# Three halvings before the column sums, quarter loads of the first two tiles, and eleven context widenings on GpSimd

## What is computed

```python
def fake_quant(x, scale, zp):
    q = jnp.clip(jnp.round(x / s + z), 0.0, 255.0)
    return (q - z) * s

x = x + tanh(g_xattn[0]) * matmul(fake_quant(layernorm(x)), fake_quant(ctx))
x = x + tanh(g_ffn[0]) * ffn(layernorm(x))     # base product, plus LoRA weighted by a top-2 router
```

## Time and profile before

| | us |
|---|---|
| median of three executions | 1054.52 |
| lowest, highest | 1052.64, 1057.77 |
| the profiled execution | 1053.84 |
| span of the profiled execution, first to last instruction | 1052.1 |
| PE busy over the span | 1018.3 (97%) |
| DVE busy | 761.2 (72%) |
| ACT busy | 482.2 (46%) |
| POOL busy | 270.8 (26%) |

### The profile page before, as it was taken

One profiled execution on the slowest core, in us unless ns is written; L12 is line 12 of the kernel. 1 busy time (PEld: TensorE's weight loads), 2 busy tenths in 40 slices (PEclk: granted clock), 3 DMA queues, 4 the chain that ended last, 5 costly groups with the idle time before them and its releaser, 6 DMA issues.

```text
span 1052.1 us, 13343 instructions
## 1 busy us (share of the span) xinstructions
PE 1018.3 (97%) x5048; PEld 769.2 (73%) x5072; DVE 761.2 (72%) x1089; ACT 482.2 (46%) x503; POOL 270.8 (26%) x331
## 2 busy tenths in 40 slices
PE   2999999999999999999989999999999999999998
PEld 1444544444888888888878888898888889888887
DVE  7879897986678553557687679968867896855654
ACT  6855885340432322234344445634444564433442
POOL 2538686789238845000000000000000000000000
PEclk9999999999999999999999999999999999999999
DMA  8795699653799998435757866867677685568665
GB/s 338 285 382 202 241 377 393 221 199 113 258 368 384 331 333 328 152 137 167 243 223 239 283 221 204 281 188 305 200 277 262 197 273 184 189 205 310 235 201 179
DMA packets 85199, 265.90 MB, mean 253 GB/s; under 512 B 7312, under 2 KB 15504, under 8 KB 77456
## 3 DMA queue, kind: packets, MB, share of 16 engines
q1 hardware_dynamic: 67472, 231.50, 62.5%
q10 hardware_dynamic: 17664, 33.56, 8.8%
HBM read 214.70 MB, written 50.33 MB: 252 GB/s over the span
## 4 chain that ended last, share of the span: by engine, by line
PE 76%; DVE 11%; DMA 6%; ACT 4%; issue 2%; SPq 0%; ACTq 0%; DVEq 0%
PE acc L1398 17%; PE acc L1400 16%; PE acc L1399 16%; PE acc L1383 15%; DMA ctx_stage<-in_ctx 3%; DVE w_lo L1091 3%; PE aT_psum L1468 2%; ACT ctx_u L761 2%; DVE S_sum L1224 1%; PE aT_psum L1446 1%; PE aT_psum L1447 1%; DVE S_lo L1232 1%; DMA w_stage<-w_sums_scratch 1%; PE aT_psum L1370 1%; DVE c_acc L1202 1%
## 5 line engine op out<-in xcount | busy, mean ns | idle before, releaser
L1091 DVE TENSOR_TENSOR w_lo<-w_stage,w_hi 128x1024 fp32r<-128x1024 f32 x200 | 247.4, 1248 | 170.3 <-ACT w_hi L811 169.5
L811 ACT ACTIVATE w_hi<-w_stage 128x1024 fp32r<-128x1024 f32 x200 | 209.6, 1059 | 335.3 <-PE acc L1400 237.0
L1398 PE MATMUL acc<-w_hi,S_hi 128*128 128x512 f32 x384 | 151.4, 394 | 2.4 <-DVE w_lo L1091 1.6
L1400 PE MATMUL acc<-w_hi,S_lo 128*128 128x512 f32 x384 | 149.7, 390 | 0.0
L1399 PE MATMUL acc<-w_lo,S_hi 128*128 128x512 f32 x384 | 149.5, 389 | 0.0
L702 POOL TENSOR_TENSOR t_job<-t_job 128x256 f32<-128x256 f32 x128 | 107.7, 872 | 56.4 <-DMA t_job<-in_wt 54.8
L1383 PE MATMUL acc<-ctx_quant,aT_even 128*128 128x512 bf16 x501 | 112.6, 382 | 2.3 <-DVE ctx_quant L1031 1.1
L1398 PE MATMUL acc<-w_hi,A_hi 128*128 128x512 f32 x288 | 114.0, 396 | 0.3
L1383 PE MATMUL acc<-ctx_quant,aT_odd 128*128 128x512 bf16 x499 | 111.1, 379 | 1.5 <-issue 0.8
L1400 PE MATMUL acc<-w_hi,A_lo 128*128 128x512 f32 x288 | 112.4, 390 | 0.0
L1399 PE MATMUL acc<-w_lo,A_hi 128*128 128x512 f32 x288 | 112.2, 390 | 0.0
(11 more groups left out here) (182 smaller groups left out, 1613.2 us busy)
## 6 DMA issues: line engine op xcount, KB each, us to landing
w_stage<-in_wt SPq DMA_DIRECT2D x104, 512.0 KB, 4.7
w_stage<-w_sums_scratch SPq DMA_DIRECT2D x96, 512.0 KB, 4.3
ctx_stage<-in_ctx SPq DMA_DIRECT2D x32, 1024.0 KB, 7.7
t_job<-in_wt SPq DMA_DIRECT2D x8, 2048.0 KB, 10.9
w_sums_scratch<-t_job SPq DMA_DIRECT2D x8, 2048.0 KB, 11.9
c_acc<-x_scratch SPq DMA_DIRECT2D x32, 512.0 KB, 5.3
out<-c_acc ACTq DMA_DIRECT2D x64, 256.0 KB, 5.4
x_rows<-x_scratch SPq DMA_DIRECT2D x11, 1024.0 KB, 8.2
```

Of the source, the lines that this page charges most:

```text
L811: ins = act.activation(wh[i % HI][:, :], raw[:, :], ACT.Copy)
L1091: ins = dve.tensor_tensor(low[:, :], raw[:, :], high[:, :].bitcast(F32), ALU.subtract)
L1398: pe.matmul(out_, lh, rh, start=first, stop=False, skip_group_check=onto)
L1400: return pe.matmul(out_, ll, rh, start=False, stop=final, skip_group_check=onto)
```

## The change

- **A third halving.** `ctx_sums` adds two of the remaining four slices to the other two, so `col_sums` has two products for a block where it had four.
- **Quarter loads.** The first two tiles are loaded in four parts of 512 columns, each with a semaphore of its own (`x_chunk`), and each `bn_stats` waits for its own part.
- **Widening on GpSimd.** `CWIDEN_POOL` names eleven of the first sixteen pieces. GpSimd widens them with the same operation, in four strips of 128x512. Who reads the pieces waits for two counters (`wait_context`).
- **All orders are written anew**: the loads, the units, which tiles ACT widens and copies, and all slots.

```diff
-LOAD_ORDER = 'xxccxcxccccccxccccxcccccxxxcxxxcccccccccxcxcxxcc'
+LOAD_ORDER = 'xxcxccxcccccccxcccccccxxxcxxccxcxccccccccxxccxcx'
-UNIT_TILE = [0, 1, 2, 2, 1, 0, 3, 3, 2, 1, 0, 3, 2, 1, 0, 3, 4, 4, 4, 5, 5, 5, 6, 7, 7, 6, 7, 6, 7, 6, 5, 4, 10,
+UNIT_TILE = [0, 1, 2, 0, 1, 2, 0, 1, 3, 3, 0, 1, 2, 4, 2, 3, 3, 4, 4, 5, 5, 6, 6, 7, 7, 5, 4, 6, 5, 7, 6, 7, 8,
...
-UNIT_BLOCK = [0, 0, 0, 1, 1, 1, 1, 2, 2, 2, 2, 3, 3, 3, 3, 0, 0, 1, 2, 0, 1, 2, 0, 0, 1, 1, 2, 2, 3, 3, 3, 3, 4,
+UNIT_BLOCK = [0, 0, 0, 1, 1, 1, 2, 2, 0, 1, 3, 3, 3, 0, 2, 3, 2, 1, 2, 0, 1, 0, 1, 0, 1, 2, 3, 2, 3, 2, 3, 3, 4,
...
-WIDEN_ACT = [0, 1, 3, 4, 5, 7, 8, 10, 11, 12, 15]
-COPY_ACT = [1, 2, 4, 5, 6, 7, 8, 9, 10, 11, 13, 14, 15]
+WIDEN_ACT = [0, 4, 5, 8, 9, 10, 11, 12, 13]
+COPY_ACT = [0, 2, 3, 4, 5, 7, 8, 9, 11, 12, 13, 14]
...
+CWIDEN_POOL = [0, 2, 3, 6, 7, 8, 9, 11, 13, 14, 15]
...
+        def wait_context(eng, q0, q1):
+            pool_pieces = [q for q in CWIDEN_POOL if q < q1]
+            if pool_pieces and pool_pieces[-1] >= q0:
+                eng.wait_ge(c_by_pool, len(pool_pieces))
+            if any(q not in CWIDEN_POOL for q in range(q0, q1)):
+                eng.wait_ge(c_by_dve, q1 - len(pool_pieces))
...
+                if t < BY_CHUNK:
+                    for c in range(NB):
+                        part = slice(c * NW, (c + 1) * NW)
+                        sp.dma_start(xg[0][:, t, part], x[t * P:(t + 1) * P, part]).then_inc(x_chunk[t][c], 16)
+                    return
...
+            def ctx_widen(q):
+                c = q // CP
+                pool.wait_ge(cu_ready, q + 1)
+                for k in range(PK * (q % CP), PK * (q % CP) + PK):
+                    ins = pool.tensor_scalar(ctxq[:, c % NB, k, :], ctxu[:, c % NB, k, :], TOP, -MID, ALU.min, ALU.add)
+                ins.then_inc(c_by_pool, 1)
...
+                if t < BY_CHUNK:
+                    for c in range(NB):
+                        dve.wait_ge(x_chunk[t][c], 16)
+                        link(dve.bn_stats(st[:, 6 * c:6 * c + 6], xg[0][:, t, c * NW:(c + 1) * NW]), wait=c == NB - 1)
...
                 dve.tensor_tensor(pair[:, 0:K // 4, :], pair[:, 0:K // 4, :], pair[:, K // 4:K // 2, :], ALU.add)\
+                    .then_inc(sums_halved, 1)
+                dve.wait_ge(sums_halved, c + 1)
+                dve.tensor_tensor(pair[:, 0:K // 8, :], pair[:, 0:K // 8, :], pair[:, K // 8:K // 4, :], ALU.add)\
                     .then_inc(sums_ready, 1)
...
-                for k in range(K // 4):
-                    ins = pe.matmul(colp[:, :], ones[:, :], pair[:, k, :], start=(k == 0), stop=(k == K // 4 - 1))
+                for k in range(K // 8):
+                    ins = pe.matmul(colp[:, :], ones[:, :], pair[:, k, :], start=(k == 0), stop=(k == K // 8 - 1))
```

More of the change, by code:

```diff
@@ L78 @@
[L78 to L84, removed]
@@ new lines @@
+STATS_SLOT = [0, 3, 12, 39, 109, 147, 188, 205, 253, 261, 325, 355, 397, 430, 461, 472]
+SCALE_SLOT = [2, 9, 22, 53, 131, 180, 200, 223, 282, 300, 339, 380, 420, 441, 467, 484]
+QUANT_SLOT = [4, 13, 28, 58, 135, 184, 207, 228, 294, 305, 349, 383, 423, 445, 471, 487]
+WIDEN_SLOT = [5, 16, 32, 74, 140, 190, 213, 234, 301, 309, 353, 386, 426, 448, 479, 495]
+ROWSUM_SLOT = [6, 20, 37, 85, 146, 199, 222, 242, 320, 321, 364, 395, 440, 458, 483, 500]
+ROWADD_SLOT = [11, 23, 43, 90, 148, 201, 226, 245, 324, 330, 366, 396, 446, 460, 486, 503]
@@ new lines @@
+CU_SLOT = [10, 19, 24, 30, 35, 47, 54, 65, 68, 72, 91, 95, 101, 111, 116, 126, 264, 271, 278, 287, 319, 334,
+    342, 356, 363, 367, 374, 379, 389, 406, 409, 418]
+CWIDEN_SLOT = [14, 25, 29, 36, 45, 57, 61, 69, 75, 81, 103, 108, 117, 125, 133, 139, 273, 279, 290, 295, 336,
+    346, 350, 361, 371, 375, 378, 384, 394, 417, 419, 424]
+SUMS_SLOT = [63, 92, 136, 162, 304, 385, 407, 444]
+COLMM_SLOT = [76, 105, 149, 176, 315, 398, 414, 454]
+COLTERM_SLOT = [86, 107, 159, 186, 323, 402, 425, 459]
+UNIT_SLOT = [42, 44, 55, 77, 78, 83, 115, 118, 121, 124, 151, 152, 160, 163, 169, 181, 191, 204, 231, 233, 243,
+    247, 259, 262, 272, 283, 293, 303, 311, 328, 338, 348, 351, 358, 368, 376, 381, 387, 390, 399, 403, 411,
+    416, 421, 427, 438, 447, 457, 462, 469, 475, 481, 491, 497, 504, 508, 514, 518, 525, 530, 536, 541, 545,
+    549]
@@ new lines @@
+EVAC_SLOT = [49, 51, 60, 79, 82, 88, 120, 122, 127, 129, 155, 157, 173, 175, 178, 183, 197, 218, 238, 240, 246,
+    248, 266, 269, 276, 289, 297, 314, 316, 333, 344, 352, 359, 369, 377, 382, 391, 392, 401, 404, 413, 415,
+    422, 428, 436, 453, 456, 465, 470, 477, 482, 494, 498, 505, 509, 515, 521, 528, 532, 538, 542, 544, 548,
+    551]
+COLADD_SLOT = [96, 99, 104, 114, 119, 144, 161, 164, 167, 171, 187, 192, 195, 208, 211, 216, 220, 232, 241, 251,
+    255, 257, 270, 275, 280, 291, 299, 317, 337, 341, 347, 354, 362, 372, 405, 408, 410, 412, 429, 431, 433,
+    439, 442, 449, 463, 466, 468, 473, 474, 480, 490, 496, 507, 510, 512, 517, 523, 531, 537, 540, 543, 546,
+    550, 552]
@@ L117 @@
+COPY_SLOT = [15, 27, 41, 84, 150, 203, 229, 244, 312, 327, 365, 393, 437, 455, 492, 506]
+STORE_SLOT = [170, 174, 225, 219, 284, 286, 370, 373, 432, 443, 451, 485, 526, 533, 547, 553]
+JOB_SLOT = [452, 478, 493, 499, 513, 519, 527, 534]
+GROUP_STATS_SLOT = [488, 501, 511, 516]
+GROUP_STD_SLOT = 520
+GROUP_RSTD_SLOT = 522
+NORMALISE_SLOT = [524, 529, 535, 539]
+SLOTS = 554
 (STATS_AT, STD_AT, SCALE_AT, QUANT_AT, WIDEN_AT, ROWSUM_AT, ROWADD_AT, CU_AT, CWIDEN_AT, SUMS_AT,
@@ L128 @@
 EARLY_H = 2
+BY_CHUNK = 2
 assert UNIT_BLOCK[-1] in (NB + 1, NB + 3)
@@ L393, in build @@
         x_in = [[sem(f"x_in{a}{m}") for m in range(M)] for a in range(2)]
+        x_chunk = [[sem(f"x_chunk{t}{c}") for c in range(NB)] for t in range(BY_CHUNK)]
         var_ready = sem("var_ready")
@@ L406, in build @@
         cu_ready = sem("cu_ready")
-        c_conv = sem("c_conv")
+        c_by_dve = sem("c_by_dve")
+        c_by_pool = sem("c_by_pool")
         block_ready = sem("block_ready")
         sums_ready = sem("sums_ready")
+        sums_halved = sem("sums_halved")
         col_ready = sem("col_ready")
@@ L711, in _ @@
                     t_step(JOB_AT[s] // 4, JOB_AT[s] % 4)
+                if s in CWIDEN_AT and CWIDEN_AT[s] in CWIDEN_POOL:
+                    ctx_widen(CWIDEN_AT[s])
                 if s in ROWADD_AT:
@@ L1101, in _ @@
                     aT_copy(COPY_AT[s])
-                if s in CWIDEN_AT:
+                if s in CWIDEN_AT and CWIDEN_AT[s] not in CWIDEN_POOL:
                     ctx_widen(CWIDEN_AT[s])
```

48 lines of the change are left out of this document (12 added, 36 removed), and 8 rows, old and new, of the table QUARTER_SLOT.

## The result

The changed kernel takes 1111.9 us (median; 1108.3 to 1112.6) against 1054.5 for the kernel before: a ratio of 1.053, 95% interval 1.051 to 1.055. The forecast was 1057.0, range 1046 to 1063, so the time lies 49 us above the range. The profiled execution, the shortest of the five, has a span of 1106.2 us, 54.1 more than before.

The account below looks back on a forecast made before the run. ScalarE sets the start, then loads, then TensorE bounds the attention part. Lost 34.1 us plus work 239.35 end it at 273.4, 2.5 later; span 1054.6, profiled 1056.3, median 1057.0 (no change), range 1046 to 1063.

Parts of the forecast that it names:

- the price of a strip: GpSimd's widening of 512 columns: taken as 0.692 us, 2.77 a piece, bounds 0.35 and 1.1.
- GpSimd's strip is dearer than 0.69: Rival on GpSimd's widenings: each 0.1 us a strip adds 3.2 us; at 1.1 the kernel takes 1070; chance 0.13.
- The clock rival: Rival: TensorE's clock falls in the three stalls for GpSimd's pieces, up to 2 us each, 1061 to 1063; chance 0.11.
- In the last stretch ... I move nothing there: Attention part's end: the two jobs' steps keep their place before unit 60, so no time was added.
- The alternation: GpSimd's strips and VectorE's halvings block each other: 4.1 us a block, TensorE stalls of 2.9, 4.5 and 3.7, together 11.1.
- the walk: Following GpSimd's order from 36.3 us: 32 us of work unblocked, piece 14 ending at 78.4 with the halvings.
- The start: First tile: root ended at 7.55, first transposes near 13.0 instead of 17.55, first unit at 19.4 instead of 23.17.
- Never waits until 45: ScalarE works without idle through conversions, quantising and copies until about 45 us, each load being there in time.
- The third halving: Column sums: sixteen products fewer, 3.45 us of TensorE gained; eight new VectorE instructions of 0.65 us.
- The 781 us: TensorE's work after the attention part, from 271 us to the end: 781.1 us, carried over unchanged.
- the forecast's own sum: Attention part: lost 34.1 against 28.2, work 239.35 against 242.8, so it ends at 273.4, 2.5 us later.

Follow-up runs that it names:

- the kernel with fast strips: Changed kernel with GpSimd's eleven pieces widened by add and mult instead of min and add, clip at 255 left out; 1061.3 us, ratio 1.006.
- the two kernels with slow strips: The changed kernel (min and add on GpSimd), ratio 1.053, and the same with the scale chain on one tensor each, 1105.4 us, ratio 1.047.
- the gap: GpSimd waits for tile 15's scale before a job step: on the changed kernel with all pieces on VectorE 1052.5 us; with add-and-mult strips on GpSimd 1057.3 us.

## Why the prediction was wrong, point by point

**The step that failed is the price of a strip.** "The nearest row is its one-input strip of 512 f32 columns, median 0.692 us, which I take", with 1.1 as upper bound. Measured: 1.919. The nearness was judged by engine, columns and number of inputs, and the worry was the conversion of types, which costs nothing (0.617 with either type). The row was an add and multiply, the change's operation is min and add, and that is what costs. The upper bound came from the same operation with waits in it, so it was no bound for another one. TensorE's waits for GpSimd were 44.9 us where the sum had 11.1. The excess is 44 x 1.23 = 54 us of an engine with no slack; between the kernel with fast strips and the one after, the ratios (1.0057 and 1.0533) are 50.2 us apart.

**The rival had the right mechanism and too small a reach.** "GpSimd's strip is dearer than 0.69", 3.2 us per 0.1, chance 0.13: by that slope 1.92 gives 1057 + 39 = 1096, still 16 us short: the slope counts the last eight pieces and leaves out the three before them, TensorE's slower pace and the wait of the last stretch. It stopped at 1070, since its price stopped at 1.1. The sum ended there for want of a row, and the range left this case out altogether.

**The Trainium skill** (GPSIMD Engine Reference, Performance versus the Vector engine) has 769 ns for 512 elements of a tight loop. Add and multiply took 617 here, below it; min took 1917, so that figure does not carry over to this operation.

**The clock rival came true as a consequence.** Its condition, stalls of TensorE, was met eleven times instead of three. Granted clock 0.78 to 0.90 in 17.5 to 150 us; eight products at 3.60 us against 1.90; +15.4 us in pace and small gaps together. The Trainium skill (TensorE: Matmul & The Clock Gate, The HAM clock gate) has the array slow again after idling; the trace agrees, and in the kernel with fast strips, whose waits for GpSimd are 2.2 us at most, the sixteen products after the wait that ended at 42.67 took 3.63 us, full pace.

**"In the last stretch ... I move nothing there"** missed 6.8 us (6.9 in the ratios of the two kernels with slow strips). In the new orders a two-tensor instruction of tile 15's scale chain waits until GpSimd's run is over. In the kernel before, the sixteen of the same line took at most 0.76 us, tile 15's 0.42 (below), where GpSimd's run (205 to 231) had no gap either. What the orders change that makes this one wait last is not found.

```profile
226.84 0.42 DVE L1002 SCALAR_TENSOR_TENSOR newton<-x_rstd,x_var_eps 128x1 f32<-128x1 f32 x1
```

**The alternation** was right in place and direction, 4.8 us of stalls instead of 11.1. GpSimd was ahead of the walk by 5.7 us at piece 14 (72.7 against 78.4): its strips' lower price is about 3 of it, and the time in which VectorE held it up, 9.9 us instead of 12.9, another 3. Of that, the halvings of blocks 0 and 1 cost 3.4 and 3.5 us instead of 4.1, and of block 2's only the first (2.0) came before piece 14 was ready.

**The start** was right but for 1.2 us: the root ended at 8.73, forecast 7.55, as the last quarters landed later (VectorE's last two statistics start at 6.54), first transposes at 14.18, forecast 13.0. ScalarE had its first tile before the context piece, as forecast. "Never waits until 45" fell with the strips.

**The third halving**: 0.69 us on VectorE undisturbed (median 1.08) for 0.65, 3.3 us on TensorE for 3.45. **The 781 us** behind the part are unchanged, to 0.1.

With its strip at 0.6 the forecast's own sum (attention part to 273.4) can be held against the kernel without the clip: 277.35, less the 6.8 of the unforeseen wait, 270.5. The walk as such was about 3 us off, in part by luck, since two of its errors have opposite signs (the start 1.2 us late, the alternation 6.3 us cheaper); the miss came from the price that it was fed.

## What to carry to other kernels

Before an elementwise step is moved to GpSimd, measure one strip of exactly that operation there, since a row with the same tile and other arithmetic can be off by a factor of three. A term that has no row of its own needs a bound that comes from a worse case, and if a sum is linear in it, the range must say what happens at twice and three times the price. When two engines contend, look at small instructions too: one on 128x1 numbers with two SBUF inputs held up three engines, and writing that chain with per-partition scalars was worth 7.6 us by the ratios (1.0022 to 0.9950, measured on different chips) and 8.3 by the marks in the traces, more than any part of the change gained. Then look where the wait went: here it moved to a place where it cost less.

## What the runs showed of the hardware that was not expected

- `tensor_scalar` on GpSimd, 128x512: add and multiply 0.62 us in either order, from uint16 or f32; min, max or subtract with a second operation 1.92 us; min alone 1.49.
- A VectorE instruction that reads two SBUF tensors waited 7.9 to 9.1 us, through eleven to thirteen GpSimd instructions, and ended within 0.03 us of the end of their run in all four kernels that show it (the kernel after, fast strips, no pieces on GpSimd, and the last of these with two one-tensor instructions). The Trainium skill (SBUF — State Buffer, SBUF: two separate sides) has the shared pair of ports locked for one whole instruction. These GpSimd instructions take about 0.7 us each, so by that rule alone the wait would be under 1 us; here it lasted for a run.
- In the other four kernels with the new orders, where the chain was rewritten or GpSimd's run had the gap, VectorE's next long wait is at the one-tensor instruction on 128x4: 4.75, 4.93, 3.44 and 3.42 us instead of 0.17, again to within 0.03 us of the end of the run. In all eight kernels GpSimd's run ended because its next step waited for a result (`x_group_odd`) behind the waiting instruction on VectorE, so GpSimd stopped only when it was out of work.
- Mostly a two-tensor instruction does not wait that long. The others of the scale chains end with the strip in flight, as that rule has it. VectorE's and GpSimd's timeline, kernel without pieces on GpSimd: the first ends at 208.85, as the four strips do.

```profile
208.22 0.63 DVE L1036 SCALAR_TENSOR_TENSOR quant_scale_bias<-x_mean_var,quant_scale_bias,scalars 128x1 f32<-128x1 f32 x1
```

```profile
206.15 2.70 POOL L697 TENSOR_SCALAR x_group_odd<-x_group_odd,row_terms 128x512 f32<-128x512 f32 x4
```

- So the theory of the experiments (an instruction with two tensors waits until the run is over, and only such) is both too wide and too narrow. Shown is that this chain passes with one tensor each, and also with two tensors and a gap in GpSimd's run. The second tensor is not what every long wait needs, as the 128x4 instruction shows, and the age of the run does not decide it either: with fast strips a two-tensor instruction 31 us into a run took 0.51 us. What makes one wait for the whole rest of a run, where most cost half a us, is open.
- A wait that the profile gives to "issue" can be three steps away from its cause, here TensorE behind ScalarE's copy, behind its quantising, behind VectorE.
